# The second image's norm in groups of 4, 2 and 1 blocks, one block's rows to a unit, and its last block on VectorE

## The reference, cut to what matters

```
x = L0(x)                       # neighbourhood attention 7x7, 8 heads, gate, then a layer norm with weights
    y = x + out * gate
    (y - mu) / sqrt(var + 1e-5) * ln_g + ln_b
t = tokens(x)
n = (t - mean) / sqrt(var + 1e-5)             # _ln_t, a second norm of the same rows, without weights
q, k = n @ Wt, n @ Wx                          # 32 columns each
h = tanh(q[:, None, :] + k[None, :, :] + bh)   # 1024 x 1024 x 32 to an image
e = h @ Wa + ba ;  a = softmax(e) ;  t = t + a @ n
t = t + ffn(_ln_t(t))                          # 8 experts, one to a token, capacity 320
```

## Time and profile before

| | |
|---|---|
| median of 3 runs | 714.52 us (714.23 to 714.83) |
| the profiled execution | 713.9 us, of which the span is 712.1 us |
| PE busy | 548.5 us, 77% |
| DVE busy | 516.3 us, 73% |
| ACT busy | 571.3 us, 80%, of it 454.9 us in 128 tanh of 3605 ns |
| POOL busy | 506.1 us, 71%, of it 413.5 us in 464 sums |
| granted PE clock, mean | 0.93 of full speed |

### The profile page before, as it was taken

One profiled execution on the slowest core, in us unless ns is written; L12 is line 12 of the kernel. 1 busy time (PEld: TensorE's weight loads), 2 busy tenths in 40 slices (PEclk: granted clock), 3 DMA queues, 4 the chain that ended last, 5 costly groups with the idle time before them and its releaser, 6 DMA issues.

```text
span 712.1 us, 12354 instructions
## 1 busy us (share of the span) xinstructions
PE 548.5 (77%) x4512; PEld 272.0 (38%) x4512; DVE 516.3 (73%) x1442; ACT 571.3 (80%) x364; POOL 506.1 (71%) x588
## 2 busy tenths in 40 slices
...
...
DMA packets 14108, 24.32 MB, mean 34 GB/s; under 512 B 1296, under 2 KB 11058, under 8 KB 13024
## 3 DMA queue, kind: packets, MB, share of 16 engines
...
...
## 4 chain that ended last, share of the span: by engine, by line
PE 32%; issue 21%; DVE 21%; ACT 17%; POOL 8%; DMA 1%; DVEq 0%; POOLq 0%; SPq 0%; ACTq 0%
ACT front L1148 15%; PE ps L895 9%; POOL front L581 5%; DVE front L1427 5%; PE ps L693 3%; PE ps L1056 3%; PE ps L1046 3%; PE ps L915 2%; DVE back L1236 2%; PE ps L722 2%; PE ps L741 2%; PE ps L732 1%; DVE back L1263 1%; POOL y_all L540 1%; PE ps L938 1%
## 5 line engine op out<-in xcount | busy, mean ns | idle before, releaser
L1148 ACT ACTIVATE front<-front 128x4096 f32<-128x4096 f32 x128 | 454.9, 3605 | 36.8 <-POOL front L581 24.9
L581 POOL TENSOR_SCALAR front<-k,q 128x1024 f32<-128x1024 f32 (+1 forms) x464 | 413.5, 908 | 42.3 <-PE ps L895 33.5
L895 PE MATMUL ps<-front,cst 128*32 128x512 f32 x2048 | 261.0, 630 | 80.4 <-ACT front L1148 73.5
L1427 DVE TENSOR_SCALAR front<-ps,q 128x512 f32<-128x512 f32 (+1 forms) x256 | 213.8, 878 | 22.0 <-PE ps L895 17.4
L895 PEld LDWEIGHTS ps<-front,cst 128*32 128x32 f32 x2048 | 55.9, 113 | 200.3 <-ACT front L1148 99.8
L1088 ACT ACTIVATE back<-back,mn 128x320 f32<-128x320 f32 (+1 forms) x128 | 62.4, 537 | 14.2 <-DVE mn L1236 14.2
L540 POOL TENSOR_SCALAR y_all<-y_all,mvs,lny 128x128 f32<-128x128 f32 x15 | 11.7, 786 | 74.2 <-DVEq L1392 58.9
L1236 DVE CUSTOM_DVE_ANT_0 back<-ps,back 128x320 f32<-128x320 f32 (+1 forms) x128 | 54.0, 469 | 12.5 <-PE ps L693 10.4
L1459 DVE COPY ptm<-ps 128x512 f32<-128x512 f32 x32 | 22.1, 692 | 38.2 <-PE ps L906 36.7
L693 PE MATMUL ps<-conv 32*128 32x320 f32 (+1 forms) x256 | 38.3, 477 | 4.9 <-DVE mn L1236 4.8
L1263 DVE COPY back<-ps 128x512 f32<-128x512 f32 x44 | 30.2, 686 | 7.5 <-PE ps L732 7.3
...
## 6 DMA issues: line engine op xcount, KB each, us to landing
...
back<-in_inner SPq DMA_DIRECT2D x1, 1280.0 KB, 10.6
...
```

The costliest lines, as they stand in the source:

```text
L581: last = nc.gpsimd.tensor_scalar(ring[u % DEPTH][:, at + lo:at + hi], k4[:, img * L + k0 + lo:img * L + k0 + hi], q4[:, m:m + 1], 1.0, ALU ...
L895: last = nc.tensor.matmul(bank(to)[c * U:(c + 1) * U, :], c_("wa", U - QPG - QPG * row, 2 * U - QPG - QPG * row), ring[t % DEPTH][:, at:at ...
L1148: nc.scalar.activation(ring[t % DEPTH], ring[t % DEPTH], ACT.Tanh).then_inc(h_ready, 1)
L1427: last = nc.vector.tensor_scalar(ring[u % DEPTH][:, at + lo:at + keys], ps[:, base + k0 + lo:base + k0 + keys], q4[:, m:m + 1], None, ALU.add)
```

## The change

The two groups of four blocks, 8 to 11 and 12 to 15, become groups of four, two and one, and block 15 is normed by DVE. The new names are steps: `rows_8` = 32, `rows_12` = 44, `rows_14` = 50 and `rows_15` = 54, each the step behind the `project_step` of a block.

| | before | after |
|---|---|---|
| blocks 8 to 11: statistics and root, on DVE | steps 32, 33 | steps 32, 33 |
| scaled rows, on POOL | all in 35 | one block each in 34 to 37 |
| weights `lng`, `lnb`, on POOL | 36, 37 | 38, 39 |
| second statistics and root, on DVE | 38, 39 | 40, 41 |
| normed rows, on POOL | all in 41 | one block each in 42 to 45 |
| blocks 12, 13 | with 14, 15 | DVE 44; POOL 45, 46, 47; DVE 48; POOL 49, 50 |
| block 14 | with 12 to 15 | DVE 50; POOL 51; DVE 52; POOL 53 |
| block 15 | with 12 to 15: DVE 52, 54; POOL 55, 56; DVE 57; POOL 58 | DVE alone, 54 and 55 |
| tokens, queries and keys of blocks 12 to 15 | 60, 61, 62 | 56, 57, 58 |
| sums of unit 64, of unit 65 | both 62 | 61, 62 |

Each `scale_rows` of one block ends in a chained wait for its own result. `SCALES` grows from six to ten entries: 33, 39, 54 and 57 become 33, 41, 44, 48, 50, 52, 54 and 55, and the first two stay.

```diff
-    gate = lambda u: FIRST if u < NEW_KEYS[1] else KEYS_1 if u < NEW_KEYS[2] else project_step(NB - 1) + 9
+    gate = lambda u: FIRST if u < NEW_KEYS[1] else KEYS_1 if u < NEW_KEYS[2] else project_step(NB - 1) + 5
...
-        middle, late_rows = project_step(11), project_step(NB - 1)
-        SCALES = (FIRST + 3, FIRST + 4,
-                  middle + 2, middle + 8, late_rows + 1, late_rows + 4)
+        rows_8, rows_12, rows_14, rows_15 = (project_step(j) + 1 for j in (11, 13, 14, 15))
+        SCALES = (FIRST + 3, FIRST + 4, rows_8 + 1, rows_8 + 9, rows_12, rows_12 + 4, rows_14, rows_14 + 2,
+                  rows_15, rows_15 + 1)
...
+                if rows_12 + 1 <= t < rows_12 + 3:
+                    scale_rows(4, t - rows_12 + 11, t - rows_12 + 12)
+                if t == rows_12 + 3:
+                    weigh_rows("lng", ALU.mult, 12, 14)
+                    weigh_rows("lnb", ALU.add, 12, 14, done=True)
+                if rows_12 + 5 <= t < rows_12 + 7:
+                    normal_rows(4, t - rows_12 + 7, t - rows_12 + 8)
+                if t == rows_14 + 1:
+                    scale_rows(5, 14, 15)
+                    weigh_rows("lng", ALU.mult, 14, 15)
+                    weigh_rows("lnb", ALU.add, 14, 15, done=True)
+                if t == rows_14 + 3:
+                    normal_rows(5, 14, 15)
...
-                if t == late_rows + 7:
+                if t == rows_15 + 2:
                     pe.wait_ge(q4_ready, 3)
                     turn_tokens(3, 3)
...
+                if t == rows_14 + 2:
+                    dve.wait_ge(ln_rows, 5)
+                    row_stats(14, 15)
+                    scale_late(t, 14, 15)
+                    dve.sem_inc(ln_last, 1)
+                    link.end()
+                if t == rows_15:
+                    dve.wait_ge(misc_read, misc_uses(t))
+                    row_stats(15, NB)
+                    scale_late(t, 15, NB)
+                    link.end()
+                    normal_rows(y_all, 15, NB)
+                if t == rows_15 + 1:
+                    weigh_rows(15, NB)
+                    row_stats(15, NB)
+                    scale_late(t, 15, NB)
+                    link.end()
+                    normal_rows(x_all, 15, NB)
+                    dve.sem_inc(t_ready[3], 1)
```

63 lines of the change are left out of this document (30 added, 33 removed).

## The result

The changed kernel took **729.63 us** (median; 728.71 to 729.69) beside 714.67 us for the kernel before on the same chip: ratio 1.0203 (1.0186 to 1.0221), so 15.0 us slower. Forecast were 6.9 us more and a range up to 727 us: the sign is right, the size less than half of what came.

What follows compares the result with a forecast made beforehand. ACT is busiest but waits for POOL's sums, taken as the bound of steps 46 to 62. The terms 2.6 + 5.7 + 0.8 + 8.3 - 11.1 + 0.6 = +6.9 us gave 721.4 us, range 711 to 727 us.

Steps and rivals of the forecast that it cites:

- A: Steps 42 to 46: DVE's step-44 root 1.6 us late plus block 13's row, +2.6 us; up to +5 at low clock.
- B: Steps 47 to 53: rows and weights moved forward on POOL, none hidden, +5.7 us.
- C: Step 53: PE's projection waits for DVE's root, delaying unit 57's sums on POOL; +0.8 us, bounds 0 and +3.2.
- the over 5 that I gave as a sign: Profile sign: PE waits over 5 us for DVE's root in steps 53 and 56, energies over 3 us behind.
- the ring's lead: DVE and PE run about 5 us ahead of POOL's own step, so a DVE piece under 5 us is free.
- D: Steps 54 to 56: DVE's norm of block 15 and the energies of unit 56 delay unit 60's sums; +8.3 us.
- M: Moment POOL could start unit 57's sums, once unit 53's energies are done; taken as 362.6 us.
- E: Steps 55 to 61: POOL's rows and key wait gone, -11.1 us; ACT's longer tanh at the front, +0.6 us.
- rival 1: Everything but POOL's own work is hidden; -4.4 us, 710.1 us; chance 0.15.
- rival 2: Half hidden: DVE starts step 54 a full lead before POOL; -0.7 us, 713.8 us; chance 0.13.
- Rival 3: Low clock behind PE's new waits makes PE pace units 42 to 56; +12.2 us, 726.7 us; chance 0.12.
- Rival 4: Block 15's two weight instructions on DVE each wait out one POOL sum; +1.8 us, 723.2 us; chance 0.05.

Runs made afterwards that it cites:

- x18: The changed kernel with the late roots of blocks 12 to 15 cut from twelve DVE instructions to two, through PSUM, giving wrong factors; 724.66 us.
- x19: The changed kernel with the late roots of blocks 12 to 14 alone cut to two instructions through PSUM, giving wrong factors; 728.19 us.
- x20: x18 with, in addition, block 15's first scaling and two weight instructions through PSUM bank 3; 720.71 us.
- x8: The kernel before with blocks 12 and 13 as their own group at the change's steps, 14 and 15 at the old ones; 721.83 us.
- x9: The changed kernel with 16 unread products on PE ahead of its waits in each of steps 49, 51 and 53; 725.98 us.
- x13: x9 with 32 more unread products on PE in step 56, ahead of the turned tokens; 725.70 us.
- x21: The changed kernel with block 15's first scaling and two weight instructions through PSUM bank 3, nothing left out; 729.17 us.
- x3: The kernel before with only block 15's rows on DVE, in steps 54 and 55; 719.26 us.
- x10: The kernel before with DVE taking more of POOL's sums from block 6 on, the norm as before; 719.59 us.
- x2: The changed kernel with block 15's second norm on DVE and its tokens, queries and keys one step later; 728.06 us.

## Why the prediction was wrong

The way of reading held: a loss at unit 50, a growing one up to unit 57, one wait before unit 60's sums, the keys' gain behind it, and then one to one to the end. Point by point:

**A, steps 42 to 46: +2.6, measured +4.4.** The place was right (POOL waits 3.44 us for the routing root instead of 1.95, and one row more). The root of step 44 has the share that I gave it, 1.6 us: with it cut, x18, x19 and x20 lose 1.4 to 2.0 us less from unit 42 to 50. What I left to my upper bound came true: behind the wait of 4.56 us in step 42 the energies took 3.64 us. But its price isn't shown: x8, in which PE has no such wait, stands at +4.4 at unit 50 as well. Where the other 1.8 us come from stays open; they are under the 2.2 us by which traces differ there.

**B and C, steps 47 to 56: +6.5, measured +10.3. This is the step that failed.** B is right: POOL's rows and weights came as priced, one 0.78, two weights of two blocks 1.28, two of one block 0.82, and with roots cut down (x18) POOL had no such wait here and lost 6.3 us from unit 50 to 57, for my 5.7. C failed: it had +0.8 us for PE's waits, with 3.2 us as its bound, where POOL waited 4.0. For step 53 alone, which it looked at, the wait was 2.33 us (PE waited 2.90 us there, not the over 5 that I gave as a sign, and its energies weren't slow). The other 1.71 us, behind the root of blocks 12 and 13 in step 48, my sum put at nothing. I had argued that "a DVE piece of under 5 us is free". But that root, those of block 14 in steps 50 and 52, and PE's slow energies behind the first two follow one another within 20 us. That the ring's lead is spent once, and that A had already eaten it, is my reading; no run takes A alone away. What the runs do show: cutting the roots (x18) takes 4.0 us off between units 50 and 57, and keeping the clock up (x9, x13) 3.5 and 3.2. Both draw on the same 4.0 us of waits. It seems to take both, the long wait and the slow energies behind it: in x18 the energies of step 51 still took 3.62 us, behind a wait of 1.40, and POOL didn't wait.

**D: the wait before unit 60's sums, +8.3, measured 9.58.** It ended at 391.02 us, 21.1 us behind M, the end of unit 53's energies (369.9), where I had 19.7: the turned tokens and their copy took 2.0 us for my 1.3, and the energies 3.64 for the 3.1 I took. From unit 57 to 60 that makes +4.0, where my terms (8.3 less the 5.6 us of POOL's first scaling and weights) make +2.7.

**E: right.** From unit 60 to 64 the gain is 4.9 us; my terms, 3.11 + 2.40 - 0.6, give 4.9.

Sum by the trace: 4.4 + 10.3 + 4.0 - 4.9 = 13.8 us, and 1.9 us that start ahead of unit 0. Of the 6.9 us that my sum lacks, 1.8 are A's, 3.2 C's, 0.6 B's and 1.3 D's.

**The rivals.** Rivals 1 and 2 are refuted by the changed kernel's own trace: the wait of 9.58 us is whole, where rival 1 had none and rival 2 3.1 us. x3 and x10, in which POOL was relieved at DVE's cost and the kernel lost, say the same, x3 with the held scaling in it. Rival 3, the low clock, is a part of the truth: energies behind the waits of steps 42, 49, 51 and 56 took 3.1 to 3.6 us, and x9 and x13 price two of these places, 49 and 51, at about 4 us; in step 53, the third that they cover, the clock was up anyway. Its 726.7 us is nearer than my forecast, and it had 0.12. Rival 4 was right in kind and wrong in its price and place: in the changed kernel's trace it costs 1 us (x21), while its neighbours with shorter roots paid 6 to 10 us, and not for the two weight instructions but for the scaling ahead of them. Block 7's 0.59 and 0.66 us don't show when that happens.

What stays open: why the changed kernel's own scaling (0.48 us) passes in the midst of POOL's eight sums, while five like it in other runs were held to the end of the row. The traces give a lead. In the changed kernel, x2, x9 and x13 it began 0.26 to 0.28 us into one of POOL's 512-column sums (0.68 us) and ended 0.1 us behind that sum's end. Four of the five held ones began within a 1024-column sum (1.1 us), the fifth 0.02 us before the end of a short one. That it is the place within POOL's instruction that decides isn't shown; no run sets it, and x2's second scaling began within a long sum and took 0.79 us.
